# TensorE's second gather of a unit moved behind the self edges and the transposes

## The reference

```
h = depthwise 7x7 convolution(x) + bias              # layer 0
h = layernorm over channels(h)
x1 = x + (gelu(h @ w1 + b1) @ w2 + b2) * layer_scale

y = affine(conv1x1(x1))                              # layer 1
nodes = y cut into 8x8 windows: 64 nodes of 24 channels each
idx = the 9 nearest nodes of each node (normalised dot product), itself among them
edge(i, j) = gelu(affine(ew @ [y_i, y_j - y_i] + eb))
h_i = max over the 9 edges                           # 48 channels
out = affine(conv1x1(h)) + x1
```

## Time and profile before

| What | Value |
|---|---|
| median of 3 runs | 1928.23 us |
| profiled execution | 1938.88 us, span 1937.1 us |
| mean granted TensorE clock | 0.927 of full speed |
| PE busy | 1693.2 us (87%) |
| DVE busy | 1354.7 us (70%) |
| ACT busy | 1083.5 us (56%) |
| L981 gathers | 4704 matmuls, 315.6 us busy, 404 ns mean |
| L947 self edges | 1568 matmuls, 187.5 us busy, 264 ns mean |
| L416 GELU of edges | 784 calls, 500.4 us busy, 696 ns mean; 347.2 us idle before them |

### The profile page before, as it was taken

One profiled execution on the slowest core, in us unless ns is written; L12 is line 12 of the kernel. 1 busy time (PEld: TensorE's weight loads), 2 busy tenths in 40 slices (PEclk: granted clock), 3 DMA queues, 4 the chain that ended last, 5 costly groups with the idle time before them and its releaser, 6 DMA issues.

```text
span 1937.1 us, 53480 instructions
## 1 busy us (share of the span) xinstructions
PE 1693.2 (87%) x17450; PEld 860.9 (44%) x17450; DVE 1354.7 (70%) x6005; ACT 1083.5 (56%) x2434; POOL 319.9 (17%) x97
## 2 busy tenths in 40 slices
PE   7999999998888888888988888888888888988886
PEld 3444444333444444444444444444444444444443
DVE  3221244333688878787878888887868787878886
ACT  0100476665566656565656666665656565656664
POOL 2000466664011111110001111111111110101110
PEclk9999699998799989899999999998989899999997
DMA  8774244444000000000000000000000000000000
GB/s 142 150 147 96 57 105 112 111 111 109 8 24 23 24 24 23 19 24 9 22 23 23 24 23 24 23 23 24 24 24 23 18 15 18 22 24 23 16 16 16
DMA packets 146108, 85.69 MB, mean 44 GB/s; under 512 B 116160, under 2 KB 143040, under 8 KB 145856
## 3 DMA queue, kind: packets, MB, share of 16 engines
q1 hardware_dynamic: 145856, 82.38, 18.7%
HBM read 53.43 MB, written 28.90 MB: 43 GB/s over the span
## 4 chain that ended last, share of the span: by engine, by line
PE 40%; DVE 25%; issue 12%; ACT 12%; SPq 8%; ACTq 1%; DMA 0%; POOL 0%; DVEq 0%; POOLq 0%
PE bank L782 8%; DVE mx L682 7%; PE bank L981 7%; DVE onehot L666 6%; DVE marked L658 5%; PE bank L971 5%; ACT gz L416 5%; SPq L222 4%; DVE t L653 4%; PE bank L947 3%; ACT pb L408 3%; PE bank L880 2%; ACT slot L433 2%; SPq L231 2%; PE bank L929 2%
## 5 line engine op out<-in xcount | busy, mean ns | idle before, releaser
L416 ACT ACTIVATE gz<-bank,gb 112x512 f32<-112x512 f32 x784 | 500.4, 696 | 347.2 <-PE bank L981 346.2
L666 DVE TENSOR_SCALAR onehot<-slot 128x256 bf16<-128x256 bf16 x1568 | 296.4, 221 | 144.3 <-PE bank L929 53.9
L336 POOL TENSOR_TENSOR rn<-nv,mhalf 128x28 f32<-128x28 f32 x28 | 145.7, 5204 | 1240.1 <-DVE onehot L666 1235.3
L981 PE MATMUL bank<-onehot,pb 64*48 64x512 bf16 x4704 | 315.6, 404 | 0.0
L682 DVE TENSOR_TENSOR mx<-gz 112x512 f32<-112x512 f32 x392 | 267.1, 682 | 41.9 <-ACT gz L416 41.6
L971 PE MATMUL bank<-yb,wd 24*64 24x512 f32 x3136 | 247.9, 682 | 50.3 <-issue 39.4
L682 DVE TENSOR_TENSOR mx<-mx 112x256 f32<-112x256 f32 (+1 forms) x784 | 277.6, 354 | 13.7
L981 PEld LDWEIGHTS bank<-onehot,pb 64*48 64x48 bf16 x4704 | 117.5, 105 | 278.9 <-issue 205.3
L325 POOL TENSOR_TENSOR rs<-ve,mhalf 112x16 f32<-112x16 f32 x56 | 162.4, 2899 | 287.5 <-DVE ve L562 287.5
L423 ACT ACTIVATE gz<-bank,gb 112x256 f32<-112x256 f32 x196 | 92.8, 473 | 196.2 <-DVE og L690 108.5
L408 ACT CAST pb<-bank 128x192 bf16<-128x192 f32 x588 | 198.9, 338 | 3.6 <-PE bank L962 3.5
(11 more groups left out here) (86 smaller groups left out, 2181.9 us busy)
## 6 DMA issues: line engine op xcount, KB each, us to landing
xrow<-in_x SPq DMA_DIRECT2D x24, 392.0 KB
ht<-conv_d SPq DMA_DIRECT2D x112, 84.0 KB
xt<-in_x SPq DMA_DIRECT2D x112, 84.0 KB
x_d<-x1o SPq DMA_DIRECT2D x112, 84.0 KB
ht<-x_d SPq DMA_DIRECT2D x112, 84.0 KB
xt<-x_d SPq DMA_DIRECT2D x56, 168.0 KB, 3.0
out<-x1o SPq DMA_DIRECT2D x224, 42.0 KB
conv_d<-x1o SPq DMA_DIRECT2D x24, 196.0 KB
```

The costliest lines, as they stand in the source:

```text
L336: nc.gpsimd.tensor_tensor(rn[:, :], nv[:, :], mhalf[:, :], ALU.pow).then_inc(s["rn_done"], 1)
L416: nc.scalar.activation(gz[:, k, t, 0:NB, :].rearrange("p k i -> p (k i)"), bank[0:OP, t, :], ACT.Gelu, bias=gb[0:OP, 0:1], scale=1.0).then ...
L666: last = nc.vector.tensor_scalar(onehot[:, k, :, t, :], slot[:, k, :, :], float(t + 1 - 99), None, ALU.is_equal)
L981: last = mm(bank[64 * c:64 * c + O, 2 * gp + u, :], pb[64 * u:64 * u + 64, k, part, 2 * gp + h, :], onehot[64 * u:64 * u + 64, k, 2 * gp + ...
```

## The change

In `pe_slot` the call of the second gather of unit n goes from its place directly behind the first one to a place behind the first `subtract`, the strip's `halfsq` or `norm` (at wx 4 and 0), the self edges and the transposes, and ahead of the second `subtract`. No instruction is added or taken away, and the other engines' programs stay as they were.

```diff
                     gather(n, k, 0)
-                    gather(n, k, 1)
                 if ahead1:
                     subtract(n + 1, 1 - k, 0, s["hi_done"], s["res1_mm"])
                 if pre and wx == 4:
...
                     self_edges(n + 1, r1 // WX, r1 % WX)
                 if ahead2:
                     transpose(n + 2, k)
+                if unit:
+                    gather(n, k, 1)
                 if ahead1:
                     subtract(n + 1, 1 - k, 1, s["mid_done"], s["res2_mm"])
```

## The result

The changed kernel is slower: 1959.78 us, the median of 4 runs (1954.18 to 1980.0), against 1930.23 us of 4 runs of the kernel before (1925.34 to 1936.21), a ratio of 1.017 (95% interval 1.012 to 1.022). The profiled execution took 1957.64 us, 18.8 us more than that of before. Slower was one of the directions held open, but 1960 lies outside the range.

A forecast was written before the change was run, and what follows sets the result against it. The VectorE-ScalarE ring was taken to bound plain slots, with TensorE entering at wx 6 and wx 0. Terms 4.3 + 7.4 - 7.5 + 0.7 = +4.9 us on the 1928.2 median gave 1933, range 1922 to 1944.

The forecast's parts named there:

- Step (4): wx 0 at a pair's head, 14 slots: marks done, nothing waits, same matmuls before `fc2`; 0, bounds -1.4 to +1.4 us.
- step (5): Granted clock: 16 falls at wx 2 vanish, -7.5 us; one more fall around the norms, +0.7, at most +4.2.
- Step (1): Plain slots: the moved gather stays hidden, second subtract still ahead of the split; 0, still 6.55 us a slot.
- the further 0.1 us a slot: Gather's weight loads behind the transposes might leave a hole in 39 slots at wx 6 and wx 0; sum about 1937.
- Step (2): wx 6, 26 slots: `fc1` 0.55 us later, `make_y` 0.21 and 0.12 late; +4.3 us, bounds +2.2 to +12.
- Step (3): wx 0 within a pair, 13 slots: norms wait for marks, `fc2` and ranks 0.65 us later; +7.4 us, bounds 6.3 to 10.
- Rival (B): The clock falls at wx 2 stay where they were: +12.4 us, 1941, slower; chance 0.28.
- (C): Rival: ScalarE uses earlier self edges at the 14 pair heads, -4.9 us; about 1923; chance 0.15.
- (D): Rival: marks ready in time, margin at wx 6 holds, clock falls as before; 1928; chance 0.12.

The follow-up runs named there:

- e2: Kernel before, with the second gather moved in slot 0 of each pair (the head) alone; 1959.47 us, ratio 1.0153.
- e17: Changed kernel, but at wx 0 the second gather behind the first subtract, ahead of the norms, plus 8 idle VectorE copies in slot 10; 1969.74 us, ratio 1.0209.
- e5: Changed kernel, with the own-node product at each pair's head issued twice; 1962.07 us, ratio 1.0189.
- e1: Changed kernel, with the old gather order put back at each pair's head alone; 1954.71 us, ratio 1.0056.
- e3: Changed kernel, with the old gather order at every wx 0; 1922.0 us, ratio 0.9966.
- e4: Kernel before, with the second gather moved at wx 2 alone; 1917.76 us, ratio 0.9945.
- e6: Kernel before, with two pairs in one loop body, so 6 restarts instead of 12; 1884.35 us, ratio 0.9778.
- e8: Kernel before, with the second gather moved at wx 2 alone and two pairs in a loop body; 1885.69 us, ratio 0.9778.
- e11: Changed kernel, with the old gather order at wx 0 and wx 6; 1917.96 us, ratio 0.9941.
- e12: Changed kernel, with the old gather order at wx 0 and 6 and two pairs in a loop body; 1872.95 us, ratio 0.9724.
- e16: The kernel of e11 with 6 idle VectorE copies in slot 10 of each pair; 1951.97 us, ratio 1.0023.
- e7: Changed kernel, with two pairs in one loop body; 1912.78 us, ratio 0.9952.
- e13: Changed kernel, with 4 idle VectorE copies in slot 10 of each pair; 1966.01 us, ratio 1.0187.
- e14: Changed kernel, with 8 idle VectorE copies in slot 10 of each pair; 1974.05 us, ratio 1.0227.
- e18: Kernel before, with the second gather at the pair's head alone moved behind the first subtract, ahead of the norms; 1937.49 us, ratio 1.0061.

## Why the prediction was wrong, step by step

Step (4), wx 0 at a pair's head, failed: "The same matmuls stand between the gather and `fc2`: 0". The matmuls are the same and nothing waits, but the step took their durations as fixed. They follow the granted clock, and their order decides how long it stays low: +2.66 us a pair, about +32 us over the 12 pairs, where at most 1.4 in all had been allowed. The earlier trace rows had both levels in them, and step (5) weighed the clock at wx 2 and wx 0 within the pair; the head, where the clock was low at every restart, was left out. e2 shows the place, e17 against after the order as the cause, e5 that a longer run ahead of the norms shortens the low even when it is only repeated work.

The heads of all these profiled executions say the same, sorted by the moment at which the clock fell, against the start of the own-node product (81 heads with the old order in before, e1, e3, e4, e6, e8, e11, e12 and e16; 49 with the new one in after, e2, e7, e13 and e14):

| fall began | low, old order, us | low, new order, us |
|---|---|---|
| 1.2 to 2.8 us ahead | 6.8 | 13.7 |
| 0.15 to 1.2 us ahead | 13.7 | 13.7 |
| 0.14 us ahead to 0.4 behind | 3.4 | none seen |
| 0.5 to 1.2 us behind | 3.4 | 10.2 |
| 1.3 to 1.6 us behind | 10.2 | 10.2 (one head) |

With 13.7 us of low the two slots took 24.2 us in either order, with 3.4 us 20.4. So the new order costs nothing at a head but the longer low, and nothing where the old one has 13.7 us too.

Step (1), plain slots, was right: 6.55 us as before, with 0.29 to 0.40 us of idle time ahead of L947. The 0.75 us taken for what is put in holds as well: from the transposes' weight loads (L938) to that of the second subtract (L962) are 1.07 us after (1350.48 to 1351.55), 0.32 before (1249.15 to 1249.47). A hole of 0.1 us behind the transposes' loads is there, but before had it too, so that the further 0.1 us a slot that led to 1937 did not come.

Step (2), wx 6, had the mechanism and too large a size. TensorE and ScalarE in a slot of wx 6 after:

```profile
1319.02 1.00 PE L947 MATMUL bank<-yb,wself 128*112 128x64 f32 x8 [0.29 <-DVE marked L658]
...
1320.92 0.94 PE L873 MATMUL bank<-ht,par 128*128 128x448 f32 x2
```

```profile
1321.56 0.33 ACT L408 CAST pb<-bank 128x192 bf16<-128x192 f32 x1
1321.90 0.72 ACT L391 ACTIVATE yb<-bank,c,par 128x448 f32<-128x448 f32 x1
```

The split in the slot of the earlier trace rows, before:

```profile
1257.38 0.33 ACT L408 CAST pb<-bank 128x192 bf16<-128x192 f32 x1
```

`make_y` starts 0.04 us behind the end of the first half of `fc1`, and 0.34 us behind the start of the split; before it was 0.21 (1257.59), so it is 0.13 us late. The slot is 0.11 us longer (8.04 to 8.15), where 0.21 and 0.12 had been put.

Step (3), wx 0 within the pair, was right in its mechanism and near in size where the clock didn't fall before. TensorE's norms and VectorE's one-hots there after:

```profile
1383.85 1.72 PE L880 MATMUL bank<-par,sq 128*128 128x4 f32 x14 [0.47 <-DVE marked L658]
...
1388.30 0.28 PE L955 MATMUL bank<-mts,prefb 128*128 128x256 bf16 x1
```

```profile
1381.62 0.36 DVE L666 TENSOR_SCALAR onehot<-slot 128x256 bf16<-128x256 bf16 x2 [1.71 <-PE bank L929]
...
1389.48 0.36 DVE L666 TENSOR_SCALAR onehot<-slot 128x256 bf16<-128x256 bf16 x2 [0.18 <-PE bank L929]
```

The norms wait for the marks, and from one-hot to one-hot are 7.86 us instead of 7.30: +0.56, with 0.47 foretold. But the falls in 7 of the slots of before are gone in after, so the mean rose by 0.10 only: +1.2 us instead of +7.4. In e1, e5 and e7 falls came in this slot: what the wait costs there hangs on the clock. That none came in after, where one more had been put, was luck for the sum.

Step (5) was right. The stretches at wx 2 after, which answer to those of the earlier trace rows:

```profile
1349.50:1352.90 3.40, 2.72 (x27) 1.69 (x27) 3.37 (x12) 2.09 (x6) 0.77 (x1) 1.00 0.20 49
1352.90:1356.30 3.40, 3.05 (x50) 1.42 (x50) 3.03 (x18) 1.79 (x5) 0.00 (x0) 1.00 0.56 138
```

TensorE is busy 2.72 us instead of 2.10, and the clock holds. It gave 0.72 + 0.12 us a pair, 10 us over the loop, where 7.5 had been put. Rival (B) fell with it. (C) came to nothing: L423 did wait less for TensorE (57.3 us for 78.5), and more for `best` (142.3 for 103.3). (D) fell with the waits for the marks.

By these steps the loop has 32 + 1 + 1 - 10 = +24 us, which but for rounding is the whole of its +24.7: no other slot changed. Without the head it would have gained some 7 us, where the sum had +4.9: the waits were put too dear and the falls a little too cheap.

Some things stay open. How the clock comes to these lengths is not shown, only that they follow the order and the moment of the fall. e1 won back less than the whole in part because at 7 of its 11 heads the fall began 0.4 to 1.1 us ahead, where both orders have 13.7 us; that the length of a pair sets this moment is suggested by e16 but not worked out. And why e18's heads take 0.7 us more at the same low is open.

## What to carry to other kernels

When a change moves work on TensorE behind a pause, ask what the run behind the pause is made of before you write a zero: here the order with all 24 gathers ahead of the tiny matmuls (four columns) had the shorter low wherever the two orders differed. A filler that closes a pause at full clock, as at wx 2, is worth trying by itself; a move can be split by slot, and each slot judged by its own distance. The mean granted clock can't be compared between two orders: what counts is whether a low stretch lies where others wait for TensorE.

## What was not expected of the hardware

A loop's restart costs TensorE 3.3 to 4.6 us of idle time and then 3.4 to 13.7 us at the lower clock (10.2 or 13.7 with the new order); halving the restarts gave some 43 us (e6, against 1927.21 us of before beside it), more than any move of an instruction here. And one kernel's executions on one core differ by 1.5% (before: 1915.77 to 1944.0 us in the 26 of 29 runs that the ratio counts; mean granted clock 0.943 in the shortest, 0.919 in one of 1943.88). The heads' lengths could make such a difference, 20 us for the first two slots of a pair with the shortest low and 24 with the longest, 11 times; that they do was not shown run by run.
